# Edge convolution on one core: a second tile picked by TensorE in every 13th chunk, three buffers for A's rows, two early fetched tiles

## What is computed

```python
h = jnp.maximum(_layernorm(x, axis=-1), 0.0)        # x: 12500 x 64, src, dst: 400000, sorted by dst
x_i, x_j = h[dst], h[src]
feat = jnp.concatenate([x_i, x_j - x_i], axis=-1)
m = jnp.maximum(feat @ W1 + b1, 0.0) @ W2 + b2
out = jax.ops.segment_max(m, dst, num_segments=12500)
return x + jnp.where(jnp.isneginf(out), 0.0, out)
```

## Time and profile before

| | |
|---|---|
| median of 3 executions | 3883.24 us |
| lowest, highest | 3880.62, 3886.99 us |
| profiled execution: time, its span | 3888.35 us, 3886.6 us |
| PE, PEld, DVE busy, share of the span | 80%, 44%, 67% |
| ACT, POOL busy | 25%, 75% |
| mean granted TensorE clock | 0.921 |
| first fill, last message product of the loop | 505.4 us, 3737.4 us |

### The profile page before, as it was taken

How to read it: one execution, slowest core, us unless ns; L and a number is a source line. 1 busy time by engine, 2 the same in 40 slices (tenths; PEclk the granted TensorE clock), 3 DMA queues, 4 the chain that set the end, 5 groups by cost and what they waited for, 6 DMA issues and landing times.

```text
span 3886.6 us, 78391 instructions
## 1 busy us (share of the span) xinstructions
PE 3121.3 (80%) x16318; PEld 1713.6 (44%) x16627; DVE 2600.9 (67%) x7920; ACT 955.2 (25%) x3840; POOL 2923.5 (75%) x3040
## 2 busy tenths in 40 slices
PE   3200079999999999999999999999999999999920
PEld 2100045555555555555555555555555555555510
DVE  5210068777777777777777777777777777777731
ACT  4420012222222222222222222222222222222200
POOL 6777777777777777777777777777777777777766
PEclk8555589999999999999999999999999999999965
DMA  9995033333333333333333333333333333333332
GB/s 367 370 415 220 27 85 96 90 93 92 90 94 92 90 93 93 90 94 92 89 95 92 90 94 92 90 95 90 90 96 90 90 93 92 90 90 96 96 88 50
DMA packets 249647, 444.05 MB, mean 114 GB/s; under 512 B 100932, under 2 KB 105913, under 8 KB 238547
## 3 DMA queue, kind: packets, MB, share of 16 engines
q1 hardware_dynamic: 91956, 221.18, 17.6%
q0 software_dynamic: 98480, 104.31, 12.9%
q10 hardware_dynamic: 58729, 113.53, 8.0%
HBM read 221.01 MB, written 217.71 MB: 113 GB/s over the span
## 4 chain that ended last, share of the span: by engine, by line
SPq 45%; issue 14%; DMA 14%; DVE 12%; POOL 8%; PE 6%; DVEq 0%; ACT 0%; POOLq 0%; ACTq 0%
SPq L337 34%; SPq L389 8%; DMA a_edges<-rows 8%; DMA a_fill<-a_edges 5%; POOL rows L462 5%; PE ps_g L775 5%; DVE state L1028 3%; DVE a_fill L997 3%; DVE dst_all L1057 3%; POOL a_rows L518 2%; DVE rows L1066 2%; SPq L411 1%; PE ps_m L794 1%; DVE rows L1014 1%; SPq L368 1%
## 5 line engine op out<-in xcount | busy, mean ns | idle before, releaser
L462 POOL DMA_INDIRECT rows<-b_table,src_idx x2717 | 2616.0, 963 | 829.2 <-issue 822.8
L775 PE MATMUL ps_g<-shared,dst_all 128*128 128x512 bf16 x11124 | 2504.6, 379 | 16.5 <-issue 0.4
L775 PEld LDWEIGHTS ps_g<-shared,dst_all 128*128 128x128 bf16 x11433 | 1106.6, 98 | 1212.8 <-issue 4.0
L997 DVE SCALAR_TENSOR_TENSOR a_fill<-a_fill,keep 128x64 f32<-128x64 f32 x3125 | 879.0, 281 | 796.2 <-DMA a_fill<-a_edges 773.3
L1028 DVE SCALAR_TENSOR_TENSOR state<-state,keep,ps_m 128x64 f32<-128x64 f32 x3125 | 863.4, 276 | 85.9 <-PE ps_m L794 39.9
L622 ACT ACTIVATE dst_all<-ident_h,key_octet 128x128 f16<-128x128 f16 x309 | 123.6, 400 | 2157.8 <-DVE state L1028 2142.9
L794 PE MATMUL ps_m<-w_diag,zt 128*128 128x128 f32 x3126 | 429.6, 285 | 145.6 <-ACT zt L655 139.1
L632 ACT ACTIVATE dst_all<-ps_g,dst_all 128x64 f32<-128x64 f32 x2472 | 539.2, 343 | 0.0
L794 PEld LDWEIGHTS ps_m<-w_diag,zt 128*128 128x128 f32 x3126 | 379.1, 192 | 278.4 <-ACT zt L655 268.5
L785 PE MATMUL ps_t<-ident,rows 128*128 128x128 f32 x1563 | 224.0, 274 | 245.5 <-DVE rows L1014 245.5
L785 PEld LDWEIGHTS ps_t<-ident,rows 128*128 128x128 f32 x1563 | 191.4, 141 | 305.8 <-DVE rows L1014 246.1
(11 more groups left out here) (123 smaller groups left out, 471.9 us busy)
## 6 DMA issues: line engine op xcount, KB each, us to landing
rows<-b_table SPq DMA_DIRECT2D x7296, 0.2 KB
a_edges<-rows SPq DMA_DIRECT2D x80, 1250.0 KB, 14.5
a_fill<-a_edges SPq DMA_DIRECT2D x312, 320.0 KB
states<-state ACTq DMA_DIRECT2D x312, 320.0 KB
rows<-b_table ACTq DMA_DIRECT2D x5376, 0.2 KB
rows<-b_table,src_idx POOLq DMA_INDIRECT x2717, 2.4
a_fill<-b_table ACTq DMA_DIRECT2D x12, 256.0 KB, 8.5
shared<-in_x_dram SPq DMA_DIRECT2D x5, 560.0 KB
```

What stands on the lines that cost most here:

```text
L462: nc.gpsimd.indirect_dma_start(out=rows[:, c % RING, t * C:(t + 1) * C], out_offset=None, in_=b_table, in_offset=at(src_idx[:, q % SRC_RIN ...
L775: last = nc.tensor.matmul(ps_g[:, half, :], key_is[:, half, g, :], table[:, g, t, :], start=(g, t) == (0, 0), stop=g == PAGES - 1)
L997: nc.vector.scalar_tensor_tensor(here, before, flag(c, 0, t), here, ALU.mult, ALU.add).then_inc(fill_step, 1)
```

## The change

Three parts, by the diff below (the full one is cut to what matters).

1. **A second pick.** In the chunks 40, 53, ..., 300 (21 of them) TensorE picks the last two tiles, so GpSimd gathers one tile fewer there. The second pick's 37 matmuls all stand at the end of TensorE's step, behind the first pick's last 16. The keys, spreads, turns, comparisons, masks and sums of such a chunk are done twice; `key_is` gets three slots and `masked` two (it lies in `blocks` now, which is free in the loop), and a mask waits for the sum before the last instead of the last. The tile fetched row by row lies one place lower in these chunks.
2. **Three buffers of A's rows.** SyncE's load of chunk c waits for `fill(c - 2, 0)`, not `fill(c - 1, 0)`.
3. **Two early tiles.** Ahead of the loop SyncE fetches tiles for chunks 19 and 20 alone (256 rows, not 384); that of chunk 18 is gathered by GpSimd. The semaphores that count fetched rows are 6, not 8.

```diff
-    AE_RING = 2
+    AE_RING = 3
+    PICKS_MOST = 2
+    TWICE_FROM, TWICE_EVERY = 40, 13
     def picks_in(c):
-        return FIRST_PICK <= c < CHUNKS
+        if not FIRST_PICK <= c < CHUNKS:
+            return 0
+        return 2 if c >= TWICE_FROM and (c - TWICE_FROM) % TWICE_EVERY == 0 else 1
+    def picks_of(c):
+        return [(picks_below(c) + i, i) for i in range(picks_in(c))]
+    KEY_RING = 3
-    HELP_EVERY, HELP_SEMS = 3, 8
+    HELP_EVERY, HELP_SEMS = 3, 6
-    EARLY = 3
+    EARLY = 2
...
-        return CHUNK - 1 - helped(c) if picks_in(c) else CHUNK
+        return CHUNK - picks_in(c) - helped(c)
...
-                if c >= 1:
-                    sp.wait_ge(fill_step, (c - 1) * CHUNK + 1)
+                if c >= AE_RING - 1:
+                    sp.wait_ge(fill_step, (c - AE_RING + 1) * CHUNK + 1)
...
             def mask(c):
-                n = pick_number(c)
-                act.wait_ge(picked, n + 1 + FREE)
-                act.wait_ge(octets_marked, c // BATCHED + 1)
-                act.wait_ge(chosen, n + FREE)
-                for o in range(OCTET):
+                for n, i in picks_of(c):
+                    act.wait_ge(picked, n + 1 + FREE)
+                    act.wait_ge(octets_marked, c // BATCHED + 1)
+                    act.wait_ge(chosen, n - 1 + FREE)
+                    for o in range(OCTET):
...
-                if picks_in(c + PICK_AHEAD):
-                    pick(c + PICK_AHEAD, range(PAGES_FIRST))
+                for n, i in picks_of(c + PICK_AHEAD)[:1]:
+                    pick(n, range(PAGES_FIRST))
...
-                if picks_in(c + PICK_AHEAD):
-                    pick(c + PICK_AHEAD, range(PAGES_FIRST, PAGES))
+                for n, i in picks_of(c + PICK_AHEAD):
+                    pick(n, range(PAGES_FIRST if i == 0 else 0, PAGES))
...
-                dve.wait_ge(picked, n - 1 + FREE)
+                    dve.wait_ge(picked, max(n - KEY_RING + 1, 0) + FREE)
...
-                    if t == CHUNK - 2 and picks_in(c + CHOOSE_AHEAD):
-                        choose(c + CHOOSE_AHEAD)
+                    for n, i in picks_of(c + CHOOSE_AHEAD):
+                        if t == CHUNK - 2 + i * LEAD:
+                            choose(c + CHOOSE_AHEAD, n, i)
```

More of the change, by code:

```diff
@@ L66, in edge_conv, with picked_tile, helped_tile @@
     FIRST_PICK = PICK_AHEAD
+    PICKS_MOST = 2
+    TWICE_FROM, TWICE_EVERY = 40, 13
     def picks_in(c):
-        return FIRST_PICK <= c < CHUNKS
-    def pick_number(c):
-        return c - FIRST_PICK
+        if not FIRST_PICK <= c < CHUNKS:
+            return 0
+        return 2 if c >= TWICE_FROM and (c - TWICE_FROM) % TWICE_EVERY == 0 else 1
     def picks_below(c):
-        return max(0, min(c, CHUNKS) - FIRST_PICK)
-    HELP_EVERY, HELP_SEMS = 3, 8
+        return sum(picks_in(d) for d in range(c))
+    def picks_of(c):
+        return [(picks_below(c) + i, i) for i in range(picks_in(c))]
+    def picked_tile(i):
+        return CHUNK - 1 - i
+    def helped_tile(c):
+        return CHUNK - 1 - picks_in(c)
+    KEY_RING = 3
+    HELP_EVERY, HELP_SEMS = 3, 6
     HELP_FROM, HELP_AHEAD = 24, 9
-    EARLY = 3
+    EARLY = 2
     SP_ROWS, ACT_ROWS = 24, (20, 20, 16)
@@ L205, in edge_conv @@
         octets = sb("octets", [P, OCTET])
[L206 to L211, removed]
+        key_bits = sb("key_bits", [P, 2, BATCHED, PICKS_MOST], I32)
+        key_octet = sb("key_octet", [P, 2, 2, BATCHED, PICKS_MOST])
+        KEY_WORDS = KEY_RING * PAGES * P // 2
+        key_is = dst_all[:, 0:KEY_WORDS].bitcast(BF16).rearrange("p (s g e) -> p s g e", s=KEY_RING, e=P)
+        behind = dst_all[:, KEY_WORDS:KEY_WORDS + P + MARKS * PICKS_MOST * OCTET]
         key_diag = behind[:, 0:P].bitcast(FP16).rearrange("p (s e) -> p s e", s=2)
[L213 to L216, removed]
+        octet_is = behind[:, P:].bitcast(F32).rearrange("p (k i o) -> p k i o", i=PICKS_MOST, o=OCTET)
+        masked = blocks[:, :, :].rearrange("p s k -> p (s k)")[:, 0:2 * OCTET * C].bitcast(F32).rearrange(
+            "p (s o c) -> p s o c", s=2, c=C)
         ps_t = psum("ps_t", [P, GROUPS, 512])
@@ L336, in fetch_row @@
             at_byte = bass.RuntimeValue.of_register_unchecked(reg, min_val=0, max_val=(N - 1) * ROW_BYTES)
-            return eng.dma_start(rows[p:p + 1, d % RING, (CHUNK - 2) * C:(CHUNK - 1) * C].bitcast(U8),
+            return eng.dma_start(rows[p:p + 1, d % RING, helped_tile(d) * C:(helped_tile(d) + 1) * C].bitcast(U8),
                                  b_bytes[:, bass.ds(at_byte, ROW_BYTES)])
@@ L364, in load_row_idx @@
             def load_row_idx(d):
-                t = d * CHUNK + CHUNK - 2
+                t = d * CHUNK + helped_tile(d)
                 n = help_number(d)
@@ L616, in spread_keys @@
             def spread_keys(c):
-                n = pick_number(c)
                 q, j = divmod(c, BATCHED)
[L620 to L623, removed]
-            def mask(c):
-                n = pick_number(c)
-                act.wait_ge(picked, n + 1 + FREE)
-                act.wait_ge(octets_marked, c // BATCHED + 1)
-                act.wait_ge(chosen, n + FREE)
-                for o in range(OCTET):
-                    last = nc.scalar.activation(masked[:, o, :], ps_g[:, n % 2, o * C:(o + 1) * C], ACT.Copy,
-                                                scale=octet_is[:, c % MARKS, o:o + 1])
-                last.then_inc(octet_masked, 1)
+                for n, i in picks_of(c):
+                    act.wait_ge(keys_split, q + 1)
+                    act.wait_ge(keys_turned, n - 1 + FREE)
+                    nc.scalar.activation(key_diag[:, n % 2, :], ident_h[:, :], ACT.Copy,
+                                         scale=key_octet[:, q % 2, 0, j, i:i + 1]).then_inc(keys_spread, 1)
+            def mask(c):
+                for n, i in picks_of(c):
+                    act.wait_ge(picked, n + 1 + FREE)
+                    act.wait_ge(octets_marked, c // BATCHED + 1)
+                    act.wait_ge(chosen, n - 1 + FREE)
+                    for o in range(OCTET):
+                        last = nc.scalar.activation(masked[:, n % 2, o, :], ps_g[:, n % 2, o * C:(o + 1) * C], ACT.Copy,
+                                                    scale=octet_is[:, c % MARKS, i, o:o + 1])
+                    last.then_inc(octet_masked, 1)
             act_regs = [act.alloc_register(f"act_row{k}") for k in range(max(ACT_ROWS))]
@@ L759, in turn_keys, with pick @@
             def turn_keys(c):
[L761 to L768, removed]
+                for n, i in picks_of(c):
+                    pe.wait_ge(keys_spread, n + 1 + FREE)
+                    pe.wait_ge(keys_matched, n - 1 + FREE)
+                    nc.tensor.matmul(ps_k[n % 2], ones_h[:, :], key_diag[:, n % 2, :], start=True, stop=True).then_inc(keys_turned, 1)
+            def pick(n, pages):
                 half = n % 2
@@ L774, in pick @@
                     for t in range(PARTS if g < PAGES - 1 else 1):
-                        last = nc.tensor.matmul(ps_g[:, half, :], key_is[:, half, g, :], table[:, g, t, :],
+                        last = nc.tensor.matmul(ps_g[:, half, :], key_is[:, n % KEY_RING, g, :], table[:, g, t, :],
                                                 start=(g, t) == (0, 0), stop=g == PAGES - 1)
@@ L990, in fill @@
                 if t == 0:
-                    before = a_fill[:, 1 - slot, W - C:W]
+                    before = a_fill[:, (slot - 1) % AE_RING, W - C:W]
                 else:
@@ L1034, in split_keys @@
                 half = q % 2
-                column = src_idx[:, q % SRC_RING, :, CHUNK - 1]
+                column = src_idx[:, q % SRC_RING, :, CHUNK - PICKS_MOST:CHUNK]
                 dve.wait_ge(src_loaded[q % SRC_RING], (q // SRC_RING + 1) * 16)
-                link(nc.vector.tensor_scalar(key_bits[:, 0, :], column, 3, None, ALU.logical_shift_right))
-                link(nc.vector.tensor_scalar(key_bits[:, 1, :], column, OCTET - 1, None, ALU.bitwise_and))
+                link(nc.vector.tensor_scalar(key_bits[:, 0, :, :], column, 3, None, ALU.logical_shift_right))
+                link(nc.vector.tensor_scalar(key_bits[:, 1, :, :], column, OCTET - 1, None, ALU.bitwise_and))
                 if q >= 2:
                     dve.wait_ge(keys_spread, picks_below((q - 1) * BATCHED) + FREE)
-                nc.vector.tensor_copy(key_octet[:, half, :, :], key_bits[:, :, :]).then_inc(keys_split, 1)
+                nc.vector.tensor_copy(key_octet[:, half, :, :, :], key_bits[:, :, :, ::-1]).then_inc(keys_split, 1)
                 dve.wait_ge(keys_split, q + 1)
@@ L1044, in split_keys @@
                     dve.wait_ge(octet_masked, picks_below((q - 1) * BATCHED) + FREE)
+                marked = (P, BATCHED * PICKS_MOST, OCTET)
                 nc.vector.tensor_tensor(
-                    octet_is[:, half * BATCHED:(half + 1) * BATCHED, :],
-                    octets[:, :].rearrange("p (k o) -> p k o", k=1).to_broadcast((P, BATCHED, OCTET)),
```

(19 more changed lines are left out.)

10 lines of the change are left out of this document (1 added, 9 removed).

## The result

| | before | after |
|---|---|---|
| median of 12 executions each, us | 3881.84 | 3892.07 |
| lowest, highest | 3878.57, 3886.99 | 3891.38, 3894.81 |
| profiled execution: time, span | 3888.35, 3886.6 | 3892.04, 3890.2 |

The changed kernel is slower by 10 us: the ratio is 1.0027, 95% interval 1.002 to 1.0035. The forecast was 3885.5 us in a range of 3856 to 3905, "no change" likeliest. The direction in the trace was forecast (2.3 us later at the loop's end), the size in the medians was not.

What follows compares the result with a forecast made beforehand. Three close limits: GpSimd's gathers, SyncE (10.41 us per chunk), TensorE (9.70). Start 19.0 us sooner, GpSimd 25 us sooner, 21 picks at 10.85 us on TensorE: end 2.3 us later, 3883.24 + 2.3 = 3885.5 us, range 3856 to 3905.

Steps and rivals of the forecast that it cites:

- Early tiles: Before the loop: with 256 early rows on SyncE, not 384, the whole loop starts 19.0 us earlier.
- The third buffer costs nothing and holds SyncE off: SyncE's loads in the loop: 28.7 us ahead, so TensorE runs at 9.70 us per chunk from the start.
- The second pick: TensorE's step in 21 double chunks: 37 matmuls take 7.98 us, a turn of keys 0.06.
- The wait of program order: TensorE, step after a double pick: next pick waits for ScalarE's mask behind the relu, 2.8 us each, about 59 in all.
- (c): Double chunks: VectorE's extra 2.9 us and ScalarE's 1.75 us of masks fit within TensorE's 11 us longer step.
- The sum: Loop's end: step 308 at 3713.7 us, last four steps 26 us, last messages at 3739.7, 2.3 us later than before.
- The first: Rival, chance 0.24: the second pick's wait is hidden or picks cost less; GpSimd's 25 us decide, 3858 us.
- The second: Rival, chance 0.14: the filled loop doesn't hold 9.70 us per step, as ScalarE's steps grow; 27 us more, 3912 us.
- The third: Rival, chance 0.07: the loop's start doesn't move, something else holding the first load; 19 us more, 3904 us.
- The rule on TensorE: Skill's headroom measure in the loop: weight loads' share, 52%, leaves nearly half free; the prediction took 56% as full.
- the four terms: The forecast's own range, 3874 to 3897 us: 8 us for the mask trip, 6 pace, 3 tail, 1 start.

Runs made afterwards that it cites:

- early3: The changed kernel with three early tiles again, not two: 3911.32 us, ratio 1.0076 to the kernel before.
- ring2: The changed kernel with two buffers of A's rows, not three: 3900.18 us, ratio 1.004 to the kernel before.
- mf_idx_act_8: mf_idx_act with a second pick in every 8th chunk, 34 in all, not every 13th: 3935.87 us, ratio 1.0141 to the kernel before.
- mask_first: The changed kernel with ScalarE masking a double chunk's first pick ahead of that step's relu, not behind it: 3869.64 us, ratio 0.9966 to the kernel before.
- mf_idx_act: mask_first with the load of the next row numbers issued by ScalarE, not SyncE: 3855.54 us, ratio 0.9927 to the kernel before.
- every26: The changed kernel with a second pick in every 26th chunk, 11 in all, not 21: 3869.72 us, ratio 0.9962 to the kernel before.
- no_twice: The changed kernel without any second pick: 3882.74 us, ratio 0.9998 to the kernel before.
- idx_act: The changed kernel with the load of the next row numbers issued by ScalarE, masks left in place: 3892.68 us, ratio 1.0026 to the kernel before.

## Why the prediction was right, and where it wasn't

- *Early tiles:* 19.0 us forecast, 20.4 in the trace (the scatters of that execution were themselves 1.2 us sooner), 19.3 by early3. GpSimd's last gather begins at 3697.7, 31 us before 3728.69. 25 were forecast; the other 6 are 2 ns less for each of 2697 gathers (mean 961 ns on the page, 963), and those 1.2 us.
- *The third buffer costs nothing and holds SyncE off:* right. In the changed kernel no step before the first double pick is late, and ring2 shows that two buffers make 14 of them late, by 8.4 us.
- *The second pick:* 37 matmuls and a turn, 8.04 us forecast, 8.04 measured in mf_idx_act_8. The wait of program order: 2.8 forecast, 21 waits of 2.48 us idle shown, 2.64 us in a step. Together 10.85 forecast, 10.63 in 18 of the cycles and 12.32 in the three with the lower clock. The mean of 10.92 is so near to 10.85 partly by luck: the forecast had the plain cycle 0.2 us too dear, 4.6 us in 21, and had no term for the clock, 5.1 us.
- *(c) the doubled work of VectorE and ScalarE stays beside TensorE:* right; TensorE's chain has neither but for the masks.
- *The sum:* step 308 forecast for 3713.7, measured 3714.27; the last four steps 26 against 26.5; the last messages 3739.7 against 3740.79.
- *The rivals:* The first was the right question with the wrong answer; mask_first shows that such a kernel exists, but it took an edit, and SyncE stood before GpSimd. The second didn't occur: 308 steps fit 9.70 us. The third didn't.
- *The rule on TensorE:* by weight loads busy 52% the picks should have been free. In mf_idx_act PE is busy for 2383.51 of 2400 us, and weight loads for 1330.06, 55%. In mf_idx_act_8 PE is busy without any gap, and weight loads have the same share, 1785.73 of 3230 us (the row below). That is full in this kernel, as 56% was in the stretch from 512 us. The measurement speaks against reading that share against 100% here.

```profile
520.00:3750.00 3230.00, 3230.00 (x17447) 1785.73 (x17446) 2515.20 (x7567) 897.90 (x3707) 2398.25 (x2497) 1.00 0.34 90
```

**The step that failed** is the one from the profiled execution to the median ("I sum differences on the span and add them to the median"). The profiled executions differ by 3892.04 - 3888.35 = 3.7 us, and the sum met that within 1.4. The medians differ by 10.2. The profiled execution of before is 6.5 us above the median of 12 and 1.4 above the highest of them; that of after is on its median. So the trace of before belongs to an execution that is some 6 us longer than usual. That the extra time lies in what SyncE and GpSimd set is argued and not shown, since no second execution of before was profiled. The new loop is counted in TensorE's steps, which its trace shows to be the same throughout but for the three, so its sum had to be set against the median of before and not against the profile: 2.3 + 6.5 = 8.8 us. Of the 6.5, 5.1 stood in the table before the forecast (3888.35 against a median of 3883.24); the other 1.4 came when 12 executions gave 3881.84. The prediction gave itself 12 us each way (the four terms that it names for this add up to 18), and the miss of 6.6 lies in that, but it gave 0.28 to "slower by over 0.2%", which is too little for a loop that it had filled to 228 of 219 us.

## What to carry to other kernels

Work is only worth moving in amounts that fit the idle time of the engine that takes it; here 228 us went into 219, and 60 of the 228 were a wait. When a step of one engine gets a second unit of work, look for the buffer that it hands on: the wait that was satisfied a step early is then in the same step, behind whatever stands ahead of it in the other engine's program, and moving three lines there was worth 22 us, and 37 together with a relief of the next queue. And a forecast against a median needs to know where the profiled execution lies among the others.

## What the runs showed that I had not expected

- The kernels differ in how closely they repeat: the changed kernel's 12 executions lie within 3.4 us and early3's 4 within 2.3, before's 12 within 8.4, every26's 4 within 10.3 and no_twice's 10 within 10.9. The wide ones are those in which SyncE sets the pace over most of the loop. It isn't a rule about who ends the loop: mf_idx_act, which GpSimd's gathers end, has 5 within 1.6 us. The profiled executions of no_twice (3887.99), every26 (3873.79) and ring2 (3902.38) are the longest of theirs and that of before is longer than all 12, those of the changed kernel, mask_first and mf_idx_act are on the median, and those of early3 and mf_idx_act_8 the shortest. Whether the profiler slows the queues of SyncE and GpSimd or this is chance was not settled.
- The granted clock fell behind some pauses of TensorE of 2.5 us and not behind others of the same length: 3 of 21 in the changed kernel and in early3, 4 of 21 in ring2 and idx_act. The kernel before, which has no such waits, has one such place too (0.64 from 2206 to 2209 us, where TensorE had been busy for only 0.99 of the 3 us ahead). What decides it stays open.
- SyncE's issue of the same 24 rows, registers and load took 10.41 us per chunk in the kernel before and 10.47 in mask_first; most of the difference is in the register loads, 1.74 us each against 1.67.
